# Two-block convolution and attention kernel: half of the last projection and half of the query transposes move in between the sets of the second depthwise convolution

## What is computed

```python
x = x + _L0_conv_ref(_gn(x), ...)   # block 0
x = x + _L1_conv_ref(_gn(x), ...)   # block 1
```

```python
qkv = jnp.einsum('bchw,oc->bohw', x, w_qkv)              # 128 -> 384 channels
y = depthwise 5x5 of qkv, then a grouped 1x1 (groups of 8)
mqkv = jnp.concatenate([qkv, y], axis=1)                  # two halves of 16 heads of 8 channels
q, k = relu(first 8), relu(next 8); v = last 8 with a row of ones
vk = jnp.einsum('bhdn,bhen->bhde', v, k)
out = jnp.einsum('bhde,bhen->bhdn', vk, q)
out = out[:, :, :-1] / (out[:, :, -1:] + ATT_EPS)         # 256 channels: first half, second half
out = jnp.einsum('bchw,oc->bohw', out, w_proj)            # the last projection, 256 -> 128
out = out * inv + (bn_beta - bn_mean * inv)               # batch norm folded into a scale and a bias
```

## Time and profile before

| what | value |
|---|---|
| median of 3 runs | 326.14 us (325.75 to 330.5) |
| the profiled execution | 326.22 us |
| span of its trace | 324.5 us |
| TensorE busy | 262.7 us, 81% of the span |
| VectorE busy | 204.5 us, 63% |
| ScalarE busy | 150.9 us, 46% |
| GpSimd busy | 122.7 us, 38% |
| sets 2 to 23 of the 5x5 convolution | from 229.99 us to about 281.45 us |
| tail | from there to 324.5 us |

### The profile page before, as it was taken

One profiled execution on the slowest core, in us unless ns is written; L12 is line 12 of the kernel. 1 busy time (PEld: TensorE's weight loads), 2 busy tenths in 40 slices (PEclk: granted clock), 3 DMA queues, 4 the chain that ended last, 5 costly groups with the idle time before them and its releaser, 6 DMA issues. The chain is left out here.

```text
span 324.5 us, 13486 instructions
## 1 busy us (share of the span) xinstructions
PE 262.7 (81%) x5763; PEld 199.7 (62%) x5763; DVE 204.5 (63%) x696; ACT 150.9 (46%) x372; POOL 122.7 (38%) x311
## 2 busy tenths in 40 slices
PE   0348799569799789966959999979898899879995
PEld 0235676348586676755647677757677777667771
DVE  3798886219996267998796766562323323458774
ACT  0456674148962568673563355330432336822220
POOL 8144664008695447744330232110223322133300
PEclk9999999859999799998799999997999999999999
DMA  7730099941002400000017082633100000001112
GB/s 232 118 81 10 18 199 204 219 121 29 4 6 47 79 3 4 2 0 1 2 40 159 19 182 56 145 75 91 36 4 4 4 4 4 5 2 51 66 50 97
DMA packets 15883, 20.07 MB, mean 62 GB/s; under 512 B 4288, under 2 KB 9408, under 8 KB 15808
## 3 DMA queue, kind: packets, MB, share of 16 engines
q1 hardware_dynamic: 12256, 18.03, 23.8%
q10 hardware_dynamic: 3568, 1.18, 2.1%
HBM read 4.33 MB, written 2.30 MB: 20 GB/s over the span
## 5 line engine op out<-in xcount | busy, mean ns | idle before, releaser
L1074 PE MATMUL bank<-cin,tband 64*32 64x240 f32 (+2 forms) x3072 | 87.8, 377 | 14.5 <-DMA cin<-cin 7.5
L1074 PEld LDWEIGHTS bank<-cin,tband 64*32 64x32 f32 x3072 | 68.7, 109 | 32.6 <-issue 13.2
L891 DVE STREAM_TRANSPOSE cpos<-bank 128x256 f32<-128x256 f32 x96 | 36.4, 423 | 52.3 <-PE bank L1074 52.1
L573 ACT ACTIVATE tband<-tband,row_edge 128x96 f32<-128x96 f32 (+1 forms) x96 | 32.4, 397 | 40.4 <-POOL tband L409 38.9
L1070 PE MATMUL bank<-ident,rings 128*128 128x128 f32 x192 | 33.0, 301 | 17.0 <-ACT rings L512 8.1
L1070 PEld LDWEIGHTS bank<-ident,rings 128*128 128x128 f32 x192 | 22.4, 150 | 29.1 <-ACT rings L512 10.7
L843 DVE STREAM_TRANSPOSE cin<-bank 128x768 f32<-128x768 f32 x32 | 30.9, 976 | 14.8 <-PE bank L1074 14.8
L445 POOL TENSOR_SCALAR ring_v<-cpos,mask_b 128x512 f32<-128x512 f32 x30 | 20.9, 708 | 35.5 <-PE bank L1074 22.4
L409 POOL TENSOR_TENSOR tband<-taps,pw 128x320 f32<-128x320 f32 x24 | 17.7, 737 | 42.6 <-PE bank L1074 42.6
L512 ACT ACTIVATE rings<-bank,ln_b,ln_s 128x128 f32<-128x128 f32 x64 | 24.2, 466 | 12.8 <-POOL ln_b L397 12.8
L445 POOL TENSOR_SCALAR ring_v<-rings,mask_b 128x512 f32<-128x512 f32 x16 | 10.9, 694 | 43.1 <-ACT rings L651 43.1
(11 more groups left out here) (131 smaller groups left out, 454.8 us busy)
## 6 DMA issues: line engine op xcount, KB each, us to landing
cin<-cin SPq DMA_DIRECT2D x48, 192.0 KB, 4.3
cin<-cin SPq DMA_DIRECT2D x40, 64.0 KB, 2.0
xin<-in_x_dram SPq DMA_DIRECT2D x4, 512.0 KB, 6.3
out_dram<-rings SPq DMA_DIRECT2D x16, 128.0 KB, 1.8
taps<-tap_rows SPq DMA_DIRECT2D x16, 60.0 KB
taps<-tap_rows SPq DMA_DIRECT2D x16, 36.0 KB
cin<-cin ACTq DMA_DIRECT2D x8, 64.0 KB
rings<-in_L_conv_w_qkv_dram ACTq DMA_DIRECT2D x1, 192.0 KB, 6.7
```

The lines of the kernel that those rows point to most:

```text
L573: last = a.activation(dst[:, :, 2 + e], dst[:, :, e], ACT.Copy, scale=row_edge[:, e:e + 1])
L891: last = v.transpose(cpos[n % NS // TS][:, :, :, g * CG:(g + 1) * CG], bank[2 * (n % 4) + q][:, 0:B * HH])
L1074: return t_.matmul(dst, stationary, moving, start=start, stop=stop, skip_group_check=True)
```

## The change

The first half's product of the last projection leaves the tail: `first_half(i)` stands after sets 3, 5, ..., 17 on TensorE and writes bank 6. VectorE adds bank 6 and the batch-norm bias to `xres` (`first_half_add`, two instructions a pair), so the eight bias activations on ScalarE go, and `final(i)` in the tail is one product instead of two. `q_transpose1(i)` stands after sets 10, 12, ..., 22 and 23 and writes bank 7; ScalarE's relu writes the transposed queries back in place of the `cpos0` that they came from (`qt1`), and `attend1` reads them there. Since banks 6 and 7 are taken, the sets of the 5x5 convolution go round three pairs of banks, and set n waits for the transposes of set n - 3. On ScalarE the last four `k_relu` now come after the last `q_out1`. The arithmetic is the same but for the order of the sums.

```diff
--- before.py
+++ after.py
@@ -60,6 +60,9 @@
 FRONT1 = 11
 X_BANKS = 0, 1, 3
 CONV1_STEPS = 8, 9
+SETS1 = 3
+FIRST_AT = tuple(range(3, 19, 2))
+QUERY_AT = 10, 12, 14, 16, 18, 20, 22, 23
 GN1 = ((0, 2, 8), (2, 5, 11), (5, 8, 13))
 TSLOTS = 4
 EPS = 1e-5
@@ -238,7 +241,8 @@
         s_div = sem("b_attn_divided")
         s_ot = sem("b_attn_transposed")
         s_half = sem("b_attn_channel_major")
-        s_xb = sem("c_residual_biased")
+        s_fp = sem("c_first_half_projected")
+        s_fa = sem("c_first_half_added")
         s_fin = sem("b_proj_done")
         s_y = sem("y_natural")
         s_out = [sem(f"out_stored_{n}") for n in ("even", "odd")]
@@ -283,6 +287,12 @@
         def unit(n):
             return banks[:, 2 * n:2 * n + 2, :].rearrange("p b n -> p (b n)").rearrange("p (l z) -> p l z", l=XL)
+
+        def set_banks(n):
+
+            return 2 * (n % 4 if n < NS else (n - NS) % SETS1)
+
+        qt1 = cpos0[:, :].rearrange("p (i n) -> p i n", i=PAIRS)
         def blocks(t):
@@ -651,13 +661,11 @@
                     a.activation(ring_d[:, i % 2, :].rearrange("p (b u m) -> p b u m", b=2, u=8)[:, :, XL * n:XL * (n + 1)],
                                  ps[:, :, UC:US].rearrange("p u (m b) -> p b u m", b=2), ACT.Relu).then_inc(s_vr, 1)
-            def q_out1(n):
-
-                act.wait_ge(s_qt1, n + 1)
-
-                act.wait_ge(s_num, PAIRS + n - 1)
-                a.activation(ring_d[:, n % 2, :].rearrange("p (b n y) -> p b n y", b=2, y=HH),
-                             bank[3][:, :].rearrange("p (n y b) -> p b n y", b=2, y=HH), ACT.Relu).then_inc(s_qc1, 1)
+            def q_out1(i):
+
+                act.wait_ge(s_qt1, i + 1)
+                a.activation(qt1[:, i, :].rearrange("p (b n y) -> p b n y", b=2, y=HH),
+                             bank[7][:, :].rearrange("p (n y b) -> p b n y", b=2, y=HH), ACT.Relu).then_inc(s_qc1, 1)
             def half_out(i):
                 act.wait_ge(s_ot, i + 1)
@@ -692,17 +700,16 @@
                 k = cpos[1][:, i].rearrange("p x c -> p (x c)")
                 a.activation(k, k, ACT.Relu).then_inc(s_k1, 1)
-            for n in range(TSLOTS, NS):
-                edges(NS + n, K1)
-                if n >= 2 * TS + TSLOTS:
+            for n in range(TSLOTS, NS + TSLOTS):
+                if n < NS:
+                    edges(NS + n, K1)
+                if n - TSLOTS in QUERY_AT:
+                    q_out1(QUERY_AT.index(n - TSLOTS))
+                if 2 * TS + TSLOTS <= n < NS:
                     k_relu(n - 2 * TS - TSLOTS)
             for i in range(PAIRS - TSLOTS, PAIRS):
                 k_relu(i)
-
-            for i in range(PAIRS):
-                last = a.activation(xres[:, i, :], xres[:, i, :], ACT.Identity, bias=bn_bias[:, :])
-            last.then_inc(s_xb, 1)
             def half1_out(i):
                 act.wait_ge(s_ot, PAIRS + i + 1)
@@ -714,8 +721,6 @@
             for step in range(PAIRS + 3):
                 if 0 <= step - 2 < PAIRS:
                     half1_out(step - 2)
-                if step < PAIRS:
-                    q_out1(step)
         @block.vector
         def _(dve):
@@ -889,7 +894,7 @@
                 for q in range(2):
                     g = 2 * (n % TS) + q
                     last = v.transpose(cpos[n % NS // TS][:, :, :, g * CG:(g + 1) * CG],
-                                       bank[2 * (n % 4) + q][:, 0:B * HH])
+                                       bank[set_banks(n) + q][:, 0:B * HH])
                 last.then_inc(s_ce, 1)
             def q_max(n):
@@ -1030,8 +1035,20 @@
                     kv_mask(n - 1)
-            for n in range(NS, 2 * NS):
-                conv_out(n)
+            def first_half_add(i):
+
+                dve.wait_ge(s_fp, i + 1)
+                for b in range(2):
+                    r = image(xres[:, i, :], b)
+                    last = v.scalar_tensor_tensor(
+                        out=r, in0=bank[6][:, b * NPOS:(b + 1) * NPOS].rearrange("p (n y) -> p n y", y=HH),
+                        scalar=bn_bias[:, :], in1=r, op0=ALU.add, op1=ALU.add)
+                last.then_inc(s_fa, 1)
+
+            for n in range(NS):
+                conv_out(NS + n)
+                if n in FIRST_AT:
+                    first_half_add(FIRST_AT.index(n))
@@ -1052,7 +1069,6 @@
                                     bank[2][:, b * NPOS:(b + 1) * NPOS].rearrange("p (l h y) -> p l h y", l=XL, h=XH),
                                     image3(xres[:, i, :], b), ALU.add).then_inc(s_y, 1)
-            dve.wait_ge(s_xb, 1)
             for step in range(PAIRS + 3):
                 if 0 <= step - 3 < PAIRS:
                     y(step - 3)
@@ -1155,8 +1171,9 @@
                 s, band = n % NS, tband[:, n % TSLOTS, :]
                 order = [ks // 2] + [k for k in range(ks) if k != ks // 2]
                 pe.wait_ge(s_tb, n + 1)
-                if s >= 4:
-                    pe.wait_ge(s_ce, n - 3)
+                slots = 4 if n < NS else SETS1
+                if s >= slots:
+                    pe.wait_ge(s_ce, n - slots + 1)
                 if n == 0:
                     pe.wait_ge(s_da, (XQ - 1) * 16 * 8)
                 if n == NS:
@@ -1169,7 +1186,7 @@
                     for j in (0, 2, 1, 3):
                         o = k * C + VARIANT[j] * QC
                         for g in range(2):
-                            dst = bank[2 * (n % 4) + g][quad(j), 0:B * HH].rearrange("p (q i n) -> p q i n", q=XQ, i=2)
+                            dst = bank[set_banks(n) + g][quad(j), 0:B * HH].rearrange("p (q i n) -> p q i n", q=XQ, i=2)
                             src = cin[half(g), s // CHUNK, SLOT[j], :, s % CHUNK].rearrange("p q (i n) -> p q i n", i=2)
                             last = product(dst[:, :, :, 2 * lo:2 * hi], band[half(g), o:o + QC],
                                            src[:, :, :, 2 * (lo + dy):2 * (hi + dy)],
@@ -1254,10 +1271,17 @@
             def q_transpose1(i):
                 if i == 0:
-                    pe.wait_ge(s_ce, 2 * NS - 2)
+                    pe.wait_ge(s_ce, NS + TS)
                 else:
                     pe.wait_ge(s_qc1, i)
-                transposes(bank[3], lambda xl: cpos[0][:, i, xl]).then_inc(s_qt1, 1)
+                transposes(bank[7], lambda xl: cpos[0][:, i, xl]).then_inc(s_qt1, 1)
+
+            def first_half(i):
+                if i == 0:
+                    pe.wait_ge(s_div, PAIRS)
+                else:
+                    pe.wait_ge(s_fa, i)
+                product(bank[6][:, :], wpt[:, 0, :], half0[:, i, :]).then_inc(s_fp, 1)
             def kv_product(n):
                 if n < PAIRS:
@@ -1296,7 +1320,8 @@
                 for b in range(2):
                     for j in range(2):
                         last = product(bank[5 + b][:, j * (C + NH1):(j + 1) * (C + NH1)],
-                                       tile(ring_d[:, n % 2, :], 2 * b + j), ctxm[:, n % 2, b, :])
+                                       tile(ring_d[:, n % 2, :] if n < PAIRS else qt1[:, n - PAIRS, :], 2 * b + j),
+                                       ctxm[:, n % 2, b, :])
                 last.then_inc(s_num, 1)
             def o_transpose(n):
@@ -1305,6 +1330,8 @@
                     pe.wait_ge(s_gn, 5)
                 else:
                     pe.wait_ge(s_half, n)
+                if n == PAIRS:
+                    pe.wait_ge(s_qc1, PAIRS)
                 transposes(bank[7], lambda xl: tile(ring_e[:, n % 2, :], xl)).then_inc(s_ot, 1)
             for step in range(FRONT1 + PAIRS + 4):
@@ -1349,30 +1376,24 @@
             pe.wait_ge(s_half, PAIRS)
             for n in range(len(CONV1_STEPS), NS):
                 conv(NS + n, K1)
-
-
-            def final(i, half):
-
-                if half == 1:
-                    pe.wait_ge(s_half, PAIRS + i + 1)
-                elif i >= 1:
+                if n in FIRST_AT:
+                    first_half(FIRST_AT.index(n))
+                if n in QUERY_AT:
+                    q_transpose1(QUERY_AT.index(n))
+
+
+            def final(i):
+
+                pe.wait_ge(s_half, PAIRS + i + 1)
+                if i >= 1:
                     pe.wait_ge(s_y, 2 * i)
-                last = product(bank[2][:, :], wpt[:, half, :], half1[:, i % 2, :] if half else half0[:, i, :],
-                               start=half == 0, stop=half == 1)
-                if half == 1:
-                    last.then_inc(s_fin, 1)
+                product(bank[2][:, :], wpt[:, 1, :], half1[:, i % 2, :]).then_inc(s_fin, 1)
             for step in range(PAIRS + 3):
                 if 0 <= step - 3 < PAIRS:
-                    if step > 3:
-                        final(step - 3, 0)
-                    final(step - 3, 1)
+                    final(step - 3)
                 if 0 <= step - 2 < PAIRS:
                     o_transpose(PAIRS + step - 2)
-                if step < PAIRS:
-                    q_transpose1(step)
-                if step == 0:
-                    final(0, 0)
```

## The result

The changed kernel took 333.83 us (median of 4 runs, 332.56 to 337.38) where the kernel before took 325.94: by the ratio 1.0275, with a 95% interval of 1.0213 to 1.0337, it is slower. 2.2 us were forecast, 7.9 were measured, and the time lies above the range. Timed again beside the experiments it had a ratio of 1.0138 (0.9918 to 1.0358) once and 1.0206 (1.0082 to 1.0329) another time, medians 329.83 and 332.23 us. The size of the loss is therefore less sure than the first interval says: these two medians lie inside the predicted range of 324.0 to 332.5 us, the first one outside it. A program shows a faster and a slower state, and the ratios compare the executions in the faster one alone, while the medians hold all.

A forecast was written before the change was run, and what follows sets the result against it. TensorE was taken to bound the kernel, with block-arrival stops in the convolution. Insertions of 12.6 us less 6.7 hidden (+5.9) and a tail 3.7 shorter gave +2.2 us, 328.4 us, range 324.0 to 332.5.

The forecast's parts named there:

- What bounds the convolution: 5x5 convolution: TensorE bounds it, with 7.23 us of stops at 256-instruction blocks, 6.7 of which would hide inserted work.
- The second rival, fixed stops: Convolution: each 256 instructions cost a fixed stop, so insertions hide nowhere; +9.1 us, 335.3 us in all; chance 0.12.
- My own rule for the arrival: Convolution: a block arrives 3.5 to 3.9 us after the block before has begun, so work up to that is free.
- The price of an insertion: Between convolution sets: a product costs 1.05 us, a group of transposes 0.60, 12.6 in all.
- my bound of 13.6: Convolution: upper bound on all insertions, eight products at 1.12 us and seven groups of transposes at 0.66.
- The sign: Whole kernel: slower, +5.9 us in the convolution and -3.7 in the tail, sum +2.2 us.
- my own deciding point: Convolution: the change is faster once insertions sum to less than 6.7 + 3.7 = 10.4 us.
- The tail: Tail: steps fall to 3.73 us and the end shortens by 0.7, 3.7 us less in all (bounds 3.0 to 5.1).
- the loop between VectorE's mask and attend: Tail steps: the next bound once TensorE has less work, 1.58 + 0.82 + 0.04 + 1.29 = 3.73 us a step.
- Work that cost "nothing" where it stood: After the last set: the eighth transposes fill TensorE's wait for masked values, cost nothing, and leave the tail's start unmoved.
- The banks, the other engines: Convolution: waits on three pairs of banks, VectorE's additions and ScalarE's moved work never end last; costed at nothing.

The follow-up runs named there:

- e1: Changed kernel plus one 128x512 product, result not read, in each of TensorE's two waits at the start of the tail; 329.88 us, ratio 1.0114 to before.
- e3: Changed kernel with the query transposes back in the tail, only the first half's product between the sets; 327.19 us, ratio 1.0011 to before.
- e5: The changed kernel timed again without any edit; 329.83 us, ratio 1.0138 to the kernel before.
- e12: Kernel before with three pairs of banks, plus an 8-column full-array product after each of sets 2 to 23; 328.75 us, one run.
- e2: Changed kernel with both halves of the last projection back in the tail, only the query transposes between the sets; 324.93 us, ratio 0.9963 to before.
- e10: Same kernel as e1, the changed kernel with a busy product in each rest, in more executions; 330.25 us, ratio 1.0192 to before.
- e9: The changed kernel again without edit, in more executions; 332.23 us, ratio 1.0206 to the kernel before.
- e11: Kernel before with the work filling TensorE's two rests at the tail's start moved behind the first attend; 328.73 us, ratio 1.0148 to before.
- e7: Kernel before with three pairs of banks for the 5x5 convolution's sets and nothing else changed; 326.53 us, ratio 1.011 to before.
- e13: Changed kernel with query transposes back in the tail and one product after each of sets 3 to 10; 330.35 us, one run.
- e4: Changed kernel with query transposes back in the tail, two products after each of sets 3, 7, 11 and 15; 325.28 us, ratio 0.9976 to before.

## Why the prediction was wrong, point by point

- **What bounds the convolution: right.** The 7.23 us of stops come with the blocks of 256 instructions, and inserted work hides in them. Of what was inserted 7.1 us were free; I had said 6.7. The second rival, fixed stops, is out: e1, e3, e5 and e12 have none or at most 0.2 us left. Its rule, that a block boundary is mostly hidden (the Trainium skill, "Runtime: NRT & Kernel Launch", "Instruction fetch mechanics"), doesn't hold in a stream of small matmuls at 25 ns each (2.00 us for 80). My own rule for the arrival, a block a fixed time after the one before has begun, was too narrow: it gave e2 a growth of 2.1 us and e3 one of 4.3, where 0.7 and 2.7 were measured, since blocks get several ahead. The changed kernel is dense enough in insertions that this made no difference there.
- **The price of an insertion: the first step that failed.** "Going back to small tiles shows no price in a row; I take none." It costs 0.20 us. Together a product costs 1.21 us, not 1.05, and transposes 0.74, not 0.60: 14.9 us and not 12.6, above even my bound of 13.6, since that bound had only the way in. The convolution grew by 7.8 us instead of 5.9. The sign was forecast right, and this is the term that makes it sure: my own deciding point was 10.4 us of insertions.
- **The tail: right in mechanism, a little off in size.** With the clock up, as in e1, e5 and e10, it is 36.15 to 36.30 us, 3.4 less than before where 3.7 were forecast. The steps of 3.70 to 3.76 us are the loop between VectorE's mask and attend (3.73).
- **Work that cost "nothing" where it stood: the second step that failed.** "It costs nothing, and the start of the tail stays where it was against the end of the convolution." The start did stay (last transposes to kv_product 2.24 us before and after). But what left the two rests had helped to keep TensorE's clock up, and no term of the sum stood for that. In the first profile the tail lost 2.2 us by it (38.47 against 36.30 in e5), in e9 1.3. That the rests lower the clock rests on the count of profiles, the pooled mean clocks and e11, not on a difference in time between e9 and e10.
- **The banks, the other engines: right** (e7, and no set waited for VectorE, ScalarE or GpSimd).

The work alone comes to +7.8 - 3.4 = +4.4 us, 1.3%, or 330.5 us on before's 326.1: inside the range. So the mis-sized terms double the forecast loss but do not by themselves carry the time to 333.83; that took the first measurement's other 3.5 us. Part of these come from the clock behind the rests (2.2 us in that profile), part, as the 1.74 us ahead of the convolution, from code that is the same in both and with no lower clock there. How much of the 3.5 belongs to each isn't settled; that the medians of the changed kernel went from 329.8 to 333.8 us between groups of runs says that the second part is not small, and that a median inside the range or outside it was in part luck.

## What to carry to other kernels

Stops of the busiest engine that are put down to "issue" and come every 256 instructions are room: work with few instructions is free there up to the sum of the stops, if it is spread over the whole stretch (e13 and e4 left a bare end and kept stops there), and beyond it each microsecond is paid in full. Price each insertion with both changes of tile size, in and out, and move only as much as the room holds and the next bound of the other stage can use: here six products in place of eight and eight groups of transposes. When work is taken out of a place where its engine waits anyway, ask what the engine's clock does there: work in a rest may earn its keep.

## What was not expected of the hardware

- A full-array product between 64x32 tiles costs 0.35 us beyond its own 0.86, and full-array transposes 0.30 beyond their 0.44; with 8 columns the whole insertion is 0.48 us.
- After slower use, some 3.4 blocks of 256 instructions went through ahead of the first stop in e13, and 3.75 in e3 with 0.2 us of stops, though in the steady bare stretch each block comes some 3.5 to 3.9 us after the one before.
- Rests of 1.8 and 1.6 us, 0.67 us apart (in e2, e3, e4 and e13 one of the two was shorter or partly filled), were followed by a stretch at half clock in six of eight profiles, and no such stretch stood there in the nine without them.
- Code that no version changed took up to 7 us more or less from one profiled execution to the next (226.90 to 234.24 us to the first transposes), so a change of 1% can't be read off one execution's total.
